# A third place for the rows of an expert's slot, in a Perceiver block with Mamba and a mixture of experts

## The reference

```
logits = einsum('btc,ec->bte', x, router_w)          # 16 experts
top_vals, top_idx = top_k(logits, 2)
gates = sigmoid(top_vals)                            # w_full: gate weights [N, E], 0 elsewhere
gate, up = split(einsum('nc,ech->neh', xf, gate_up_w))   # 512 wide each
out_all = einsum('neh,ehc->nec', silu(gate) * up, down_w)
moe = einsum('ne,nec->nc', w_full, out_all)
shared = einsum('bts,cs->btc', silu(sg) * su, shared_down_w)
return moe + shared                                   # and the residual
```

## Time and profile before

| | |
|---|---|
| median of 3 runs | 2560.06 us (2557.88 to 2561.17) |
| the profiled execution | 2556.76 us, its span 2555.0 us |
| busy share: PE, DVE, ACT, POOL | 94%, 77%, 63%, 27% |
| mean TensorE clock granted | 0.979 |
| stage `experts` | from 2253 us of the span to its end |
| its slots, first and last transposes of rows | 2293.89 and 2502.82 us |
| data moved in the span | 366.02 MB, mean 143 GB/s |

### The profile page before, as it was taken

One profiled execution on the slowest core, in us unless ns is written; L12 is line 12 of the kernel. 1 busy time (PEld: TensorE's weight loads), 2 busy tenths in 40 slices (PEclk: granted clock), 3 DMA queues, 4 the chain that ended last, 5 costly groups with the idle time before them and its releaser, 6 DMA issues. The chain is left out here.

```text
span 2555.0 us, 39407 instructions
## 1 busy us (share of the span) xinstructions
PE 2400.3 (94%) x14143; PEld 1015.5 (40%) x14143; DVE 1979.3 (77%) x1982; ACT 1605.8 (63%) x1973; POOL 679.0 (27%) x468
## 2 busy tenths in 40 slices
PE   7999999999999799999999999999787778988998
PEld 3333333333333244444444444444332234444444
DVE  5777777777777788888889888888679983358886
ACT  5555555565564477887878787887374432238884
POOL 1455555565554400000000000000049970020001
PEclk9999999999999899999999999999889899999999
DMA  6244644554444683343434343332340013168993
GB/s 247 83 149 159 206 161 148 170 172 161 150 153 131 165 232 96 102 109 89 107 90 105 85 115 98 96 102 67 113 166 1 0 66 132 50 234 341 379 378 126
DMA packets 177959, 366.02 MB, mean 143 GB/s; under 512 B 19490, under 2 KB 90275, under 8 KB 174179
## 3 DMA queue, kind: packets, MB, share of 16 engines
q1 hardware_dynamic: 176290, 360.75, 44.5%
q0 software_dynamic: 1280, 4.20, 0.5%
q10 hardware_dynamic: 322, 0.21, 0.0%
HBM read 254.24 MB, written 106.68 MB: 141 GB/s over the span
## 5 line engine op out<-in xcount | busy, mean ns | idle before, releaser
L452 DVE TENSOR_REDUCE kv_mx<-kv_s 128x1024 f32 (+1 forms) x512 | 595.6, 1218 | 224.2 <-PE kv_s L488 224.2
L795 DVE TENSOR_TENSOR at_pl<-at_pf,at_ph 128x1024 f16<-128x1024 f32 x512 | 613.2, 1223 | 115.8 <-ACT at_ph L742 106.9
L748 ACT ACTIVATE at_pf<-at_st 128x1024 f32<-128x1024 f32 x512 | 497.7, 1026 | 189.0 <-PE at_st L913 184.9
L912 PE MATMUL at_st<-keep_big,at_k_cur 128*128 (+1 forms) x1024 | 391.0, 382 | 11.7 <-DMA at_k_one<-kd 9.2
L913 PE MATMUL at_st<-keep_big,at_k_one 128*128 (+1 forms) x1024 | 389.4, 380 | 0.0
L742 ACT ACTIVATE at_ph<-at_pf 128x1024 f16<-128x1024 f32 x256 | 273.0, 1066 | 0.0
L1107 POOL MEMSET mamba_zero<- 128x2 f32 x1 | 0.1, 100 | 946.1 <-POOLq L60 946.1
L876 PE MATMUL at_acc<-at_ph,at_vs 128*128 128x512 f16 x1024 | 242.6, 379 | 3.0 <-DVE at_pl L795 2.9
L368 POOL TENSOR_TENSOR kv_ksl<-kv_kf,kv_ksh 128x512 f16<-128x512 f32 x128 | 148.0, 1156 | 247.0 <-ACT kv_ksh L396 247.0
L1021 PE MATMUL kv_kp<-first_ch,first_wkh 128*128 128x512 f16 x512 | 195.4, 382 | 4.5 <-DVEq L434 4.5
L1021 PE MATMUL kv_kp<-first_ch,first_wkl 128*128 128x512 f16 x512 | 195.2, 381 | 0.0
(11 more groups left out here) (357 smaller groups left out, 3882.7 us busy)
## 6 DMA issues: line engine op xcount, KB each, us to landing
keep_big<-gate_up SPq DMA_DIRECT2D x17, 2048.0 KB, 9.7
at_k_cur<-kd SPq DMA_DIRECT2D x128, 256.0 KB, 3.8
at_vs<-vd SPq DMA_DIRECT2D x64, 512.0 KB, 3.9
vd<-kv_vs SPq DMA_DIRECT2D x15, 2048.0 KB, 7.7
kv_tf<-wpack SPq DMA_DIRECT2D x21, 1024.0 KB, 9.1
keep_big<-down SPq DMA_DIRECT2D x17, 1024.0 KB
first_cf<-ctxT SPq DMA_DIRECT2D x16, 1024.0 KB, 12.7
at_k_one<-kd SPq DMA_DIRECT2D x64, 256.0 KB, 4.4
```

The source lines that it names most:

```text
L452: nc.vector.reduce_max(mx[:, bass.ds(g * (NH * TT) + 2 * (m - TT), 2)], s1[:, m % 3, :, :], AX.X).then_inc(s1_max, 1)
L748: nc.scalar.activation(pf[:, s % FULL, :, :], st[:, s % HP % NST, :, :], ACT.Exp, scale=SCORE).then_inc(pf_ready, 1)
L795: nc.vector.tensor_tensor(pl[:, s % RING, :, :], pf[:, s % FULL, :, :], ph[:, s % RING, :, :], ALU.subtract).then_inc(pl_ready, 1)
L912: nc.tensor.matmul(st[:, w % NST, e, :], k_cur[:, tile], qh[:, q], start=True, stop=False)
```

## The change

A third tile `xr2` and a third semaphore for it. Ahead of the loop the rows of three slots are loaded; iteration s of SP's loop issues the rows of slot s + 3 where it issued those of slot s + 2, so the rows of each slot from 3 on are issued one iteration sooner. The wait on `sx_ready` asks for the same count in iteration s as before (s + 1). No other engine's order changes, and the same bytes move.

```diff
-        xr = [m.sb(f"xr{i}", [P, 2 * D], F16) for i in range(2)]
+        RX = 3
+        xr = [m.sb(f"xr{i}", [P, 2 * D], F16) for i in range(RX)]
...
-                if s >= 2:
-                    sp.wait_ge(sx_ready, s - 1)
-                sp.dma_start(xr[s % 2][:, :], xs_dram[own_slot(s), :]).then_inc(x_in[s % 2], 16)
+                if s >= RX:
+                    sp.wait_ge(sx_ready, s - RX + 1)
+                sp.dma_start(xr[s % RX][:, :], xs_dram[own_slot(s), :]).then_inc(x_in[s % RX], 16)
...
-            load_rows(0)
-            load_rows(1)
+            for s in range(RX):
+                load_rows(s)
...
-                if s + 2 < SLOTS:
-                    load_rows(s + 2)
+                if s + RX < SLOTS:
+                    load_rows(s + RX)
...
-                pe.wait_ge(x_in[s % 2], 16 * (s // 2 + 1))
+                pe.wait_ge(x_in[s % RX], 16 * (s // RX + 1))
```

More of the change, by code:

```diff
@@ L1690, in experts @@
         g_in, d_in = ([m.sem(f"{n}{i}") for i in range(3)] for n in ("g_in", "d_in"))
-        x_in = [m.sem(f"x_in{i}") for i in range(2)]
+        x_in = [m.sem(f"x_in{i}") for i in range(RX)]
         w_in, made, consts = m.sem("w_in"), m.sem("made"), m.sem("consts")
@@ L2129, in rows @@
                 for c in range(2 * DC):
-                    last = nc.tensor.transpose(sxt[:, c, :], xr[s % 2][:, c * P:(c + 1) * P], ident16[:, :])
+                    last = nc.tensor.transpose(sxt[:, c, :], xr[s % RX][:, c * P:(c + 1) * P], ident16[:, :])
                 last.then_inc(sx_ready, 1)
```

## The result

| | before | changed |
|---|---|---|
| median, this comparison | 2561.17 us (5 runs, 2557.88 to 2565.63) | 2539.27 us (5 runs, 2538.53 to 2539.58) |
| ratio | | 0.9917, 95% interval 0.9905 to 0.9929 |
| the profiled execution, its span | 2556.76, 2555.0 us | 2538.53, 2536.8 us |

The change gains 21.9 us between the medians, and 18.2 us between the two profiled executions. The two differences, 21.9 and 18.2, are the first thing to explain, and one of the errors lies there.

The account below looks back on a forecast made before the run. The prediction took the ring through the load of rows as the bound, then the DMA queue at 395 GB/s: 2556.76 - 14.5 = 2542.3 us for the profiled execution, 2545.6 against the median 2560.06; range 2542 to 2552.5.

Parts of the forecast that it names:

- The ring through the load of rows: SP's load of rows queues behind a store waiting for ACT, PE and the load before; PE's waits total 14.5 us.
- the free slots: Transposes of slots 2, 3 and 4, taken as unwaited: 8.65 and 8.74 us apart, mean 8.70 against 9.64.
- The 2 us of waits: PE's waits for rows in the changed kernel, if any, come only in the last slots, some 2 us together.
- The lead of 13.2 us: After the change a load of rows may take about 13.2 us from its issue before PE waits.
- the two edits costed at nothing: Third load of rows ahead of the loop, 0.65 us if uncovered, and the `sx_ready` wait, which never holds SP.
- the unchanged tail: From the last transposes to the end only the last stores are waited for, so the tail moves as it is.
- The rate of the DMA queue: In the slots the queue rises from 384 to 395 GB/s as dry places fill; last rows come 14.5 us earlier.
- the DMA term (14.5): At 395 GB/s the rows of slot 22 are there at 2488.3 us, 14.5 us earlier than before.
- PE's (16.9): From slot 4 to slot 22, 18 periods at 8.70 us take 156.6 instead of 173.48 us: 16.9 us less.
- 384 GB/s: Rival: loads keep their old mean rate and waits for rows return about halfway; gain 9.5 us, 2550.6 us; chance 0.28.
- spreading slow stretches: Rival: with more queued, 375 GB/s gains 5.1 us, 370 gains 2.6, no change; chance 0.07 shared with another rival.
- a lower rate: Rival: backlog lowers the queue's rate; at 350 GB/s over the stage 8.1 us later, 2568.2 us; chance 0.03.

Follow-up runs that it names:

- two kernels: Changed kernel with rows issued behind the gates and down weights, 2546.12 us; changed kernel with one more 256 KB load per iteration, 2552.17 us.
- three profiles of a ring: Kernel before, profiled at 2556.76 and 2562.25 us; three places with the rows of slot s + 2 still issued in iteration s, profiled at 2554.01 us.
- the kernel with 256 KB more: Changed kernel with one more 256 KB load in each iteration, ahead of the rows, into a tile nobody reads: 2552.17 us.
- the second profile: The kernel before, profiled once more with no edit: 2562.25 us, span 2560.5.
- a kernel with waits of 7 us: Kernel before, two places, with its loads of rows moved behind the gates and down weights of set s + 5: 2724.14 us, one run.
- the additions later: Changed kernel with all four additions of the shared half in slot 0 moved behind the second pair of gate splits: 2539.78 us.
- the additions spread: Changed kernel with one addition of the shared half in each of slots 0 to 3, behind the second gate splits: 2537.67 and 2537.48 us.

## Why the prediction missed

Right, by its own steps:
- The ring through the load of rows was the bound, its share in the chain overstated the gain, and the period falls to that of the free slots with no other wait behind it. The 2 us of waits that it expected in the last slots did not come.
- The queue is served in order, and the bytes ahead of a load decide when it lands. With 404 GB/s it gave the time of slot 22 in two kernels to within 1 us (2491.8 expected and 2492.4 measured, 2496.7 and 2496.2).
- The lead of 13.2 us, the growth of the landing time to 12.2, the two edits costed at nothing, the unchanged tail.

Wrong, against the 2542.3 us that it gave for the profiled execution, where 2538.5 were measured:
- **The rate of the DMA queue (2.4 us).** The prediction let the queue bind, at 395 GB/s, and took its 14.5 us for the gain. "The slow stretches with the share at 1 I take as the traffic's own, and leave them." They were not: in the eight profiles with the same traffic whose rows are issued sooner than in the ring, the changed kernel's among them, the queue moved 403 to 405 GB/s from 2330 to 2490 us. The old mean could be no measure of what the queue can do: a ring whose slots take 9.64 us moves 3.67 MB / 9.64 us = 381 GB/s, also where the queue could do more, and a share of 1.01 did not show that. With 404 the last rows are there before PE asks for them, and the DMA term (14.5) gives way to PE's (16.9), which the prediction had beside it as its upper bound.
- **The period of the free slots (0.85 us).** It took the mean of 8.65 and 8.74, and 18 periods at 8.65 make the difference. The second was no free slot: PE's row at 2329.34 has no wait, but the weight load that goes with it has one of 0.41 us for the rows, so slot 4 was in the ring already. The changed kernel repeats 8.65 in each.

```profile
2329.34 0.45 PEld L2130 LDWEIGHTS ex_gp<-ex_ident,ex_xr 128*128 128x128 f16 x8 [0.41 <-DMA ex_xr<-xs_dram]
```

- 0.4 us by which the slots began sooner in this execution.

Against the median the miss is 6.3 us, and its largest part is another step: "**against the median 2560.06 the same gain gives 2545.6**". That carries the 3.3 us between the profiled execution and the median over to the changed kernel. In the three profiles of a ring that there are (spans 2552.3, 2555.0 and 2560.5 us) slots 4 to 22 took 170.3, 173.5 and 177.4 us and the rest of the span 2382.0, 2381.5 and 2383.1: nearly all of the scatter is loss in the ring, longer waits and falls of the clock behind the longest. The change removes that part. It does not remove the fall between slots 1 and 2, 1.7 us in one of the three. That the 3.3 us of the median are of the same kind is inferred from these three; no execution at the median was profiled. So the time of the new kernel should have been set against the profiled execution alone. With the two terms above put right as well that is 2556.76 - 16.9 - 0.85 = 2539.0, where 2539.27 was measured; with the prediction's own 14.5 it would still have been 3.0 us too high. For the same reason the range ended too high: its lower end subtracted a gain of 18 from a median that had more than 18 to give. A gain of over 17 had 0.03 of the chances, under the condition that ACT and PE do better than in the slots taken as free; that is what the gain of 17.7 us in the slots was.

Of the rivals, 384 GB/s, spreading slow stretches and a lower rate did not occur. The Trainium skill's 425 GB/s for a core alone (HBM Reference, Specifications (TRN2)) was not reached either, with 403 to 405 here, but its consequence, that the loads keep up and 16.9 us hold, was nearer than mine.

What stays open: which descriptors or rings left engines idle in the slow stretches of the first half, where SP's issue was only 0.5 to 1 us late. The runs show that they vanish once the rows are issued sooner or behind more bytes, not how.

## What to carry to other kernels

A load that sits in a ring (issue behind a store that waits for the result of the load before) shows as a long DMA piece in the chain; its price is PE's wait, and what an earlier issue brings is worked out from the bytes ahead of it in its queue. The rate to use is that of stretches with a real backlog, not the mean of a queue that is fed just in time, however busy its engines look. If the loss varies from run to run and the change removes it, as in this one case, take the new time from the profiled execution and the free pieces in it, not from the median less the gain.

## What the runs showed of the hardware

- Over the stage, a busy share of the DMA engines of 1.00 to 1.03 went with 377 to 391 GB/s in the three profiles of a ring, and 1.03 to 1.04 with 403 to 405 in the others; 402 GB/s had 1.03 too. A share at 1 did not tell a queue at its full rate from one some per cent below it.
- With the largest backlog SP's issue of one load of rows took 1.25 us instead of 0.43, and of a store 1.26 instead of 0.34 (2374 to 2378 us of the kernel with 256 KB more).
- PE's granted clock fell to 0.50 behind both waits of over 2 us among the slots of the second profile, and cost 1.7 us each in the slot after; behind the wait of 2.35 us ahead of slot 1's gate product, which all profiles have, it fell in two of the 13 and not in the others. In a kernel with waits of 7 us it fell in each slot.
- The changed kernel, which waits for no load in the slots, has a spread of 1.1 and 1.8 us in two comparisons of 5 runs each; the kernel before, in the same two, 7.8 (5 runs) and 9.6 (8 runs). Two other kernels without such waits scatter by 3.7 us (the additions later, 4 runs) and 4.3 (the additions spread, 5 runs), so not all scatter comes from the ring.
